# The scaling of a finished sum moved amid the fourth group's relus, and a last stage whose normalise precedes the seventh block's output rows

## Chip, cores and metric

The kernel runs on one core of a Trainium2 chip. The metric is the device time of one execution in microseconds (us), the median of several runs. Everything is fp32 unless said otherwise.

## What is computed

x has 4096 rows (tokens) of 128 values; adj is a 4096 x 4096 matrix. Four residual branches follow each other:

```python
x = x + gnn0(layernorm(x), adj)          # two layers of a normalised graph aggregation
x = x + ffn0(layernorm(x))               # 8 experts, top-1 routing, capacity 640
x = x + adj @ (layernorm(x) * W)         # third stage: one plain aggregation
h = relu(layernorm(x) @ Wi.T + bi)       # fourth: 64 segments of 64 tokens
for l in range(2):                       # each segment has one expert of 16
    h = relu(h @ Ws[l] + bs[l] + h @ Wr[l, e].T + br[l, e] + h)
x = x + h @ Wo.T + bo
```

The change is in the last stage of the kernel, which computes the last two branches together.

## The kernel before, in words

Each engine has its own program, written out by hand; they are tied together by semaphores only. Nothing is planned by a scheduler, so the order on each engine is the order in the code. TensorE's instructions run in program order, and so do those of VectorE (DVE), ScalarE (ACT), GpSimd (POOL) and SyncE (SP), which starts most DMAs.

In the last stage the 4096 tokens are cut into NB = 8 blocks of BW = 512. For each block k (1 to 8 here) the kernel aggregates columns of adj over all 4096 rows into the PSUM bank PA[1]; scales the sum by W while it copies it to SBUF (`oT`); turns it to token rows with four 128 x 128 transposes (`turn_sum`, bank T[0]); adds the residual (`x3`), takes the moments, normalises (`hn3`); turns it back (`turn_hn3`); computes h0; runs two routed layers; and projects out (`out_proj`) to give rows that are stored to `out`.

The aggregation of blocks 1 to 7 (numbers of `split_block`) uses a 2 x 2 scheme with seven products: `first_pairs`, `cross_pairs`, `right_pairs`, `left_pairs`, each over four quarters of the block's 8 MB. VectorE makes the combinations of matrix blocks that they stream (`sum_forms`, `cross_forms`, `second_forms`, `third_forms`), and after the last quarter it makes one more addition (`add_outer`), which a few small products on TensorE (`select`) put into PA[1]. `select` of block k runs after `first_pairs` of the first quarter of block k + 1. After it come `cross_pairs`, and then `right_pairs` of block k + 1, which starts a new sum in PA[1] and so waits (on `s_oT`) until ScalarE has taken out the finished one.

Work on two blocks is interleaved: while block k is aggregated, the routed layers of the block before it run between its quarters. The routed layers work in four groups g of four segments: groups 0 and 1 are layer 0, groups 2 and 3 are layer 1. `routed` makes the products of a group into one bank of LB = [SR, SM, O[0], O[1]]; VectorE copies them to SBUF (`raw_rows`, L1542), TensorE transposes them (`turn_routed`, L2149) into T[0] for even and T[1] for odd groups, and ScalarE applies bias and relu (L847), two instructions for each of the 16 segments n, since each has the bias of its own expert, whose number ScalarE loads first (L841). The scaling of the finished sum (L828) is ScalarE's first instruction of the next step, behind all 16 segments. `out_proj(k)` waits for these relus (`s_l`).

The last step (`last3` on TensorE, `last_hn3` on VectorE, `last_inputs` on ScalarE) has no next block to hide behind. It works in two halves of 256 tokens: `select`, the scaling by VectorE (L1566) in two halves, `turn_sum_half` into T[0] and T[1], addition (L1571) and moments on VectorE, the power for 1/sqrt on GpSimd (L875, L878), the normalise (L1580), `turn_hn3_half` (L2089), ScalarE's copy (L801), `h0_half` (L2095), ScalarE's relu into `h_a` (L805), then the two layers (`layer`, L2140) and the last `out_proj` (L2162). `keep_warm` issues products whose results nobody reads. Between the turned sum and the normalise stand, for the seventh block, `out_proj(NB - 1)` on TensorE and `out_rows3(NB - 1)` (L1672) on VectorE; the latter releases GpSimd's store of those rows (L974), and GpSimd's addition of the output bias (L979) comes behind that store.

SyncE loads the quarters of adj (L446, 2 MB each) and 16 expert matrices for each block (L642, 256 KB each) as TensorE releases the buffers.

Of the kernel before, what the change touches and what calls it, by code (L numbers as in the profile page):

```python
# [25 lines left out]
ALU = mybir.AluOpType  # L26
# [5 lines left out]
P = 128  # L32
# [51 lines left out]
def build(nc, A, out):  # L84
    ctx = ExitStack()
    with ctx:
# [121 lines left out]
        def x3_of(k):  # L208
            return (x3_even, x3_odd)[k % 2]
# [54 lines left out]
        def turned(k, g, pair, m):  # L264
            if k == NB:
                return (T, PA)[g % 2][m][:, pair * P:(pair + 1) * P]
            return T[g % 2][:, (pair * KH + m) * P:(pair * KH + m + 1) * P]

        b_last = small[:, 48:48 + L2 * KH * SB].rearrange("p (lm s) -> p lm s", lm=L2 * KH, s=SB)
        raw = [U[:, KH * BW + BW * i:KH * BW + BW * (i + 1)] for i in range(2)]  # L270

# [412 lines left out]
        def _(act):  # L684
# [112 lines left out]
            def last_inputs():  # L797

                for h in range(2):
                    act.wait_ge(s_hn3p, NB + h)  # L800
                    nc.scalar.copy(hT3[:, h * HW:(h + 1) * HW], T[h][:, h * HW:(h + 1) * HW]).then_inc(s_hT3, 1)  # L801
                for h in range(2):
                    act.wait_ge(s_h0p, NB + h)
                    for m in range(KH):
                        last = nc.scalar.activation(h_a[:, m * BW + h * HW:m * BW + (h + 1) * HW], O[h][:, m * HW:(m + 1) * HW],  # L805
                                                    ACT.Relu, bias=b_i[:, m:m + 1])
                    last.then_inc(s_h0, 1)
                for g in range(NG):
                    act.wait_ge(s_la, g + 1)
                    alone(act)  # L810
                    rows = group_rows(g, 0)
                    nc.scalar.activation(rows, rows, ACT.Relu).then_inc(s_l, 1)

            def step3(k, slot, rnd, prev, nxt):

                if not prev:

                    for s in range(SB):
                        e = act.value_load(route_sb[0:1, ds((NB - 1) * SB + s, 1)], min_val=0, max_val=E2 - 1)
                        last = nc.scalar.copy(b_last[:, :, s:s + 1], b_r.rearrange("p (lm e) -> p lm e", lm=L2 * KH, e=E2)[:, :, ds(e, 1)])  # L820
                    last.then_inc(s_bl, 1)
                    return
                if k == NB:
                    last_inputs()
                    return
                act.wait_ge(s_agg3, k)
                act.wait_ge(s_oTt, k)
                nc.scalar.activation(oT, PA[1][:, :], ACT.Copy, scale=w_g[:, 0:1]).then_inc(s_oT, 1)  # L828
                act.wait_ge(s_hn3p, k)
                nc.scalar.copy(hT3, T[1][:, :]).then_inc(s_hT3, 1)  # L830
                act.wait_ge(s_h0p, k)
                for m in range(KH):
                    last = nc.scalar.activation(h_a[:, m * BW:(m + 1) * BW], O[m][:, :], ACT.Relu, bias=b_i[:, m:m + 1])
                last.then_inc(s_h0, 1)
                for n in range(L2 * SB):
                    l, s = n // SB, n % SB
                    dst = (h_b, h_a)[l]
                    if n == SB and k in SPLIT:
                        act.wait_ge(s_cross, k)
                        nc.scalar.copy(Eh, PA[0][:, 0:SW]).then_inc(s_e, 1)  # L840
                    e = act.value_load(route_sb[0:1, ds((k - 1) * SB + s, 1)], min_val=0, max_val=E2 - 1)  # L841
                    if s % SH == 0:
                        act.wait_ge(s_rt, (k - 1) * NG + n // SH + 1)
                        alone(act)
                    for m in range(KH):
                        src = turned(k, n // SH, s % SH // 2, m)[:, s % 2 * SEG:(s % 2 + 1) * SEG]
                        last = nc.scalar.activation(dst[:, m * BW + s * SEG:m * BW + (s + 1) * SEG], src, ACT.Relu,  # L847
                                                    bias=b_r[:, ds(e + (l * KH + m) * E2, 1)])
                    if s % SH == SH - 1:
                        last.then_inc(s_l, 1)  # L850
# [144 lines left out]
        def _(dve):  # L995
# [563 lines left out]
            def last_hn3():  # L1559

                x3 = x3_of(NB)
                dve.wait_ge(s_agg3, NB)
                alone(dve)
                for h in range(2):
                    at = slice(h * HW, (h + 1) * HW)
                    nc.vector.tensor_scalar(oT[:, at], PA[1][:, at], w_g[:, 0:1], None, ALU.mult).then_inc(s_oT, 1)  # L1566
                for h in range(2):
                    at = slice(h * HW, (h + 1) * HW)
                    dve.wait_ge(s_oTt, NB + 1 + h)
                    alone(dve)  # L1570
                    nc.vector.tensor_tensor(x3[:, at], T[h][:, at], R[:, ds((NB - 1) * BW + h * HW, HW)], ALU.add)  # L1571
                    dve.drain()
                    stats(lambda t: x3[:, t * D:(t + 1) * D], (h + 1) * H2, h * H2).then_inc(s_mv4, 1)
                out_rows3(NB - 1)
                for h in range(2):
                    dve.wait_ge(s_rstd4, NB + h)
                    alone(dve)
                    for t in range(h * H2, (h + 1) * H2):
                        c = slice(t * D, (t + 1) * D)
                        last = nc.vector.tensor_scalar(hn3[:, c], x3[:, c], mv8[:, t, 0:1], rstd[:, t:t + 1], ALU.subtract, ALU.mult)  # L1580
                    last.then_inc(s_hn3, 1)
                dve.wait_ge(s_bl, 1)
                alone(dve)
                for l in range(L2):
                    for g in (2 * l, 2 * l + 1):
                        raw_rows(NB, g)
                    for g in (2 * l, 2 * l + 1):
                        relu_rows(NB, g)
# [75 lines left out]
            def out_rows3(k):  # L1664
                dve.wait_ge(s_x3b, k)
                alone(dve)
                if k > 1:
                    dve.wait_ge(s_stored, (k - 1) * 16)
                    alone(dve)
                dve.wait_ge(s_fin, k)  # L1670
                alone(dve)
                nc.vector.tensor_tensor(ob, SR[:, :], x3_of(k), ALU.add).then_inc(s_out, 1)  # L1672
                dve.drain()

            def split_step(k):
# [54 lines left out]
        def _(pe):  # L1730
# [347 lines left out]

            def turn_sum_half(h):
                pe.wait_ge(s_oT, NB + 2 + h)  # L2080
                pe.wait_ge(s_l, (NB - 1) * NG - 1 + h)
                for t in range(h * H2, (h + 1) * H2):
                    last = nc.tensor.transpose(T[h][:, t * P:(t + 1) * P], oT[:, t * P:(t + 1) * P], ident[:, :])
                last.then_inc(s_oTt, 1)

            def turn_hn3_half(h):
                pe.wait_ge(s_hn3, NB + h)
                for t in range(h * H2, (h + 1) * H2):
                    last = nc.tensor.transpose(T[h][:, t * P:(t + 1) * P], hn3[:, t * P:(t + 1) * P], ident[:, :])  # L2089
                last.then_inc(s_hn3p, 1)  # L2090
# [29 lines left out]
            def routed(k, g):  # L2120

                l, half = g * SH // SB, g % (SB // SH)
                src = (h_a, h_b)[l]
                if g == 0:
                    pe.wait_ge(s_h0, k)
                    pe.wait_ge(s_out, k)
                elif g == 1 and k == NB:
                    pe.wait_ge(s_h0, NB + 1)
                if l == 1:
# [22 lines left out]
            def out_proj(k):  # L2152
                if k < NB:
                    pe.wait_ge(s_l, k * NG)
                for t in range(BT):
# [3 lines left out]
                    for kk in range(KH):  # L2159
                        for h in range(2):  # L2160
                            at = kk * BW + t * P + h * HC
                            mm = nc.tensor.matmul((T[t // 2] if k == NB else SR)[h * HC:(h + 1) * HC, t * D:(t + 1) * D], h_a[:, at:at + HC],  # L2162
                                                  w_o[:, kk * D:(kk + 1) * D], start=kk == 0, stop=kk == KH - 1)
                    if t == BT - 1 or k == NB and t == 1:
                        mm.then_inc(s_fin, 1)
# [2 lines left out]
            def layer(k, l):  # L2168
                routed(k, 2 * l)
                routed(k, 2 * l + 1)  # L2170

            def split_block(k):
# [31 lines left out]
                cross_pairs(k, 3)  # L2204
                layer(k, 1)
                right_pairs(k, 3)
                turn_routed(k, 2)
                turn_routed(k, 3)
                left_pairs(k, 3)

            def last3(k):
                select(NB - 1)
                turn_sum_half(0)
                turn_sum_half(1)
                out_proj(NB - 1)
                keep_warm(1, S[:, 0:BW], PA[0])
                turn_hn3_half(0)
                keep_warm(1, S[:, 0:BW], PA[0])
                turn_hn3_half(1)
                h0_half(0)  # L2220
                h0_half(1)
                layer(k, 0)
                turn_routed(k, 0)
                turn_routed(k, 1)
# [78 lines left out]
```

## Time and profile before

| | |
|---|---|
| median of 3 runs | 1010.72 us (1010.53 to 1011.39) |
| the profiled execution: its time, its span | 1009.27 us, 1007.5 us |
| mean granted clock of TensorE | 0.99 of 2.4 GHz |
| last stage, aggregation of seven blocks | from about 700 to 979 us of the span |
| a block in its steady state | 40.8 us, TensorE busy 39.45 us |
| from the start of the last two layers to the end | 990.89 to 1007.5 us |

The span runs from the first to the last instruction of the profiled execution; times in the rows count from its start. A busy time is that of the engine's instructions; TensorE's matmuls overlap in the records, and one matmul of fp32 shows as two records. PEld is the load of weights into TensorE. The idle time in brackets behind a row is that of the engine ahead of this instruction, with what ended it. SR, SM, T, O and PA are PSUM banks.

### The profile page before, as it was taken

What the parts mean: (1) busy time and instruction counts of PE and PEld (TensorE: products, weight loads), DVE (VectorE), ACT (ScalarE), POOL (GpSimd) and SP (SyncE); (2) the same over time, 40 slices, a digit from 0 to 9 for tenths busy, and PEclk for the clock granted to TensorE, in tenths of its full rate; (3) what the DMA queues carried; (4) which work ended last, traced back from release to release, by engine and by line L of the source; (5) the groups of instructions that cost most, each with busy time, mean ns of one, the idle gap of its engine ahead of it and who ended that gap; (6) DMA issues with size and microseconds to landing.
All of it is one profiled execution on the core that took longest, in us unless ns stands there. A gap on an engine that the chain in (4) does not pass through costs nothing.

```text
span 1007.5 us, 15493 instructions
## 1 busy us (share of the span) xinstructions
PE 977.2 (97%) x4946; PEld 565.9 (56%) x4946; DVE 496.7 (49%) x1458; ACT 310.3 (31%) x606; POOL 188.8 (19%) x216
## 2 busy tenths in 40 slices
PE   8999999999999999999998999989999999999988
PEld 4555555555555444444444588735666666666655
DVE  6323233223223243344343487676775765756634
ACT  3654654654641010000000244322223223132231
POOL 3110010010010121212221156551120120201101
PEclk9999999999999999999999899989999999999998
DMA  9995685375204698888878259349989898898650
GB/s 358 421 408 180 283 334 206 139 324 230 105 0 168 255 335 309 313 313 320 310 265 329 81 179 297 119 155 365 375 318 336 293 342 305 320 327 292 233 168 23
DMA packets 64479, 262.74 MB, mean 261 GB/s; under 512 B 8836, under 2 KB 24904, under 8 KB 52102
## 3 DMA queue, kind: packets, MB, share of 16 engines
q1 hardware_dynamic: 61254, 257.16, 68.2%
q0 software_dynamic: 2864, 4.39, 1.3%
q8 instruction: 39, 0.64, 0.3%
q14 instruction: 50, 0.41, 0.1%
q10 hardware_dynamic: 272, 0.13, 0.0%
HBM read 243.85 MB, written 20.01 MB: 262 GB/s over the span
## 4 chain that ended last, share of the span: by engine, by line
PE 83%; DVE 4%; ACT 3%; issue 3%; ACTq 2%; DMA 2%; DVEq 2%; POOL 1%; SPq 0%; POOLq 0%
PE PA L1768 22%; PE PA L1788 22%; PE PA L2025 13%; PE O L1963 3%; PE O L2140 3%; PE O L1837 3%; ACTq L841 2%; ACT U L778 2%; PE SR L2162 1%; PE O L1809 1%; PE SR L2140 1%; PE SM L2140 1%; PE O L1799 1%; PE O L2117 1%; PE T L2149 1%
## 5 line engine op out<-in xcount | busy, mean ns | idle before, releaser
L1788 PE MATMUL PA<-ring,S 128*128 128x512 f32 x512 | 229.9, 595 | 1.7 <-DMA ring<-in_adj_cols 1.7
L1768 PE MATMUL PA<-ring,U 128*128 128x512 f32 x512 | 226.7, 595 | 0.0
L1768 PEld LDWEIGHTS PA<-ring,U 128*128 128x128 f32 x512 | 94.8, 190 | 106.6 <-issue 106.5
L1788 PEld LDWEIGHTS PA<-ring,S 128*128 128x128 f32 x512 | 95.2, 190 | 103.2 <-issue 100.4
L2026 PE MATMUL PA<-ring 128*64 128x256 f32 x560 | 133.0, 381 | 0.0
L698 ACT ACTIVATE work<-ring 128x2048 int8<-128x2048 f32 x64 | 122.2, 1910 | 8.9 <-issue 4.7
L2025 PE MATMUL PA<-ring,S 128*64 128x256 f32 x448 | 105.3, 380 | 0.3 <-DVE ring L1626 0.3
L2025 PE MATMUL PA<-ring 128*64 128x256 f32 x336 | 82.5, 382 | 7.8 <-ACT work L828 7.8
L2025 PEld LDWEIGHTS PA<-ring,S 128*64 128x64 f32 x448 | 60.5, 137 | 35.4 <-issue 6.4
L2026 PEld LDWEIGHTS PA<-ring 128*64 128x64 f32 x560 | 75.0, 137 | 0.0
L2025 PEld LDWEIGHTS PA<-ring 128*64 128x64 f32 x336 | 44.4, 137 | 33.9 <-ACT work L828 10.6
L2026 PE MATMUL PA<-U,S 128*64 128x256 f32 x224 | 54.5, 381 | 0.0
L956 POOL DMA_INDIRECT y_d<-R,work x40 | 45.4, 1134 | 46.0 <-DVE R L1438 35.7
L1184 DVE TENSOR_TENSOR U<-O,b_us 128x256 f32<-128x256 f32 x16 | 6.8, 425 | 90.6 <-PE O L1837 90.6
L875 POOL TENSOR_SCALAR small<-mv 128x4 f32<-128x4 f32 (+1 forms) x9 | 2.1, 234 | 259.2 <-DVE mv L1003 259.2
L1616 DVE TENSOR_TENSOR ring<-ring 128x1024 f32<-128x1024 f32 x28 | 34.2, 1222 | 33.2 <-PE PA L2026 33.0
L944 POOL DMA_INDIRECT disp_d<-work x32 | 31.9, 997 | 94.0 <-DVE work L1360 86.7
L847 ACT ACTIVATE work<-T,work 128x64 f32<-128x64 f32 x112 | 29.0, 310 | 63.4 <-PE T L2149 50.8
L847 ACT ACTIVATE U<-T,work 128x64 f32<-128x64 f32 x112 | 29.1, 310 | 51.8 <-PE T L2149 37.5
L1626 DVE TENSOR_TENSOR ring<-ring 128x1024 f32<-128x1024 f32 x28 | 38.4, 1373 | 2.6
L711 ACT ACTIVATE work<-work,small 128x256 f32<-128x256 f32 x32 | 16.6, 588 | 68.4 <-POOL small L908 68.4
L748 ACT COPY work<-T 128x512 f32<-128x512 f32 x8 | 4.7, 586 | 106.0 <-PE T L1873 106.0
(292 smaller groups left out, 1366.9 us busy)
## 6 DMA issues: line engine op xcount, KB each, us to landing
ring<-in_adj_cols SPq DMA_DIRECT2D x52, 2048.0 KB, 8.7
ring<-in_adjT_cols SPq DMA_DIRECT2D x32, 2048.0 KB, 8.7
ring<-w_d SPq DMA_DIRECT2D x128, 256.0 KB, 3.9
ring<-in_adj_cols SPq DMA_DIRECT2D x8, 1024.0 KB, 13.1
ring<-in_Wr SPq DMA_DIRECT2D x4, 2048.0 KB, 9.4
w_d<-ring SPq DMA_DIRECT2D x8, 1024.0 KB
work<-in_w SPq DMA_DIRECT2D x16, 256.0 KB
disp_d<-U SPq DMA_DIRECT2D x4, 650.0 KB, 20.0
```

The costliest lines, as they stand in the source:

```text
L698: last = nc.scalar.activation(junk, src, ACT.Gelu, scale=GELU_SCALE, accum_out=csum[slot][:, col:col + 1])
L847: last = nc.scalar.activation(dst[:, m * BW + s * SEG:m * BW + (s + 1) * SEG], src, ACT.Relu, bias=b_r[:, ds(e + (l * KH + m) * E2, 1)])
L944: nc.gpsimd.indirect_dma_start(disp_d, bass.IndirectOffsetOnAxis(ap=idx[:, t:t + 1], axis=0), rows[:, t * ROW:(t + 1) * ROW], None, bounds ...
L956: nc.gpsimd.indirect_dma_start(y_d, bass.IndirectOffsetOnAxis(ap=e_idx[par][:, q:q + 1], axis=0), e_y[par][:, q * D:(q + 1) * D], None, bo ...
L1616: nc.vector.tensor_tensor(S1[c % 2], q21, q22, ALU.add).then_inc(s_form, 1)
L1626: nc.vector.tensor_tensor(S2[c % 2], S1[c % 2], q11, ALU.subtract).then_inc(s_form, 1)
L1768: mm = nc.tensor.matmul(out_T[:, :], X[:, t * D:(t + 1) * D], ring[slot][t // HT][:, (t % HT) * BW:(t % HT + 1) * BW], start=n == 0, stop= ...
L1788: mm = nc.tensor.matmul(PA[k % 2][:, :], S[:, t * D:(t + 1) * D], ring[slot][t // HT][:, (t % HT) * BW:(t % HT + 1) * BW], start=t == 0, s ...
L1837: mm = nc.tensor.matmul(o, h1T[:, f * BW + t * P:f * BW + (t + 1) * P], W_us[:, f, :], start=f == 0, stop=f == KH - 1)
L2025: nc.tensor.matmul(bank[0:HC, cols], low, low_in, start=start, stop=False, skip_group_check=True)
L2026: return nc.tensor.matmul(bank[HC:P, cols], high, high_in, start=start, stop=False, skip_group_check=True)
L2140: mm = nc.tensor.matmul(LB[g][c * SEG:(c + 1) * SEG, pair * DH:(pair + 1) * DH], src[:, kk * BW + s * SEG:kk * BW + (s + 1) * SEG], wst[n0 ...
```

## The change

1. On ScalarE the scaling of the sum of block k + 1 (numbers of ScalarE's steps) is now issued in step k, ahead of segment n = 14 of 16, so two segments' relus come behind it. Step 1 issues its own at its head.
2. In the seventh block `left_pairs` of the last quarter goes ahead of the transposes of groups 2 and 3.
3. In the last step `turn_sum_half` writes O[0] and O[1] in place of T[0] and T[1] and no longer waits for the relus of the seventh block; `turn_hn3_half` has that wait now.
4. `out_proj(NB - 1)` moves behind `h0_half(1)`, with its result in PA[0] in place of SR; `out_rows3(NB - 1)` moves behind the normalise; the keep-warm products write PA[1], and there are three in place of one ahead of the first `turn_hn3_half`.
5. h0 of the last step goes to a buffer of its own, `h_last`, since `out_proj(NB - 1)` still reads `h_a`; and the first routed products of the last step no longer wait for the seventh block's output rows.

```diff
+        h_last = ring[1][0][:, 0:KH * BW]
...
-                        last = nc.scalar.activation(h_a[:, m * BW + h * HW:m * BW + (h + 1) * HW], O[h][:, m * HW:(m + 1) * HW],
+                        last = nc.scalar.activation(h_last[:, m * BW + h * HW:m * BW + (h + 1) * HW], O[h][:, m * HW:(m + 1) * HW],
...
+            def scaled_sum(k):
+                act.wait_ge(s_agg3, k)
+                act.wait_ge(s_oTt, k)
+                nc.scalar.activation(oT, PA[1][:, :], ACT.Copy, scale=w_g[:, 0:1]).then_inc(s_oT, 1)
...
-                act.wait_ge(s_agg3, k)
-                act.wait_ge(s_oTt, k)
-                nc.scalar.activation(oT, PA[1][:, :], ACT.Copy, scale=w_g[:, 0:1]).then_inc(s_oT, 1)
+                if k == 1:
+                    scaled_sum(1)
...
+                    if n == L2 * SB - SH // 2 and k + 1 < NB:
+                        scaled_sum(k + 1)
...
-                    nc.vector.tensor_tensor(x3[:, at], T[h][:, at], R[:, ds((NB - 1) * BW + h * HW, HW)], ALU.add)
+                    nc.vector.tensor_tensor(x3[:, at], O[h][:, at], R[:, ds((NB - 1) * BW + h * HW, HW)], ALU.add)
...
-                out_rows3(NB - 1)
                 for h in range(2):
                     dve.wait_ge(s_rstd4, NB + h)
...
                     last.then_inc(s_hn3, 1)
+                out_rows3(NB - 1)
...
-                nc.vector.tensor_tensor(ob, SR[:, :], x3_of(k), ALU.add).then_inc(s_out, 1)
+                nc.vector.tensor_tensor(ob, (PA[0] if k == NB - 1 else SR)[:, :], x3_of(k), ALU.add).then_inc(s_out, 1)
...
             def turn_sum_half(h):
                 pe.wait_ge(s_oT, NB + 2 + h)
-                pe.wait_ge(s_l, (NB - 1) * NG - 1 + h)
...
-                    last = nc.tensor.transpose(T[h][:, t * P:(t + 1) * P], oT[:, t * P:(t + 1) * P], ident[:, :])
+                    last = nc.tensor.transpose(O[h][:, t * P:(t + 1) * P], oT[:, t * P:(t + 1) * P], ident[:, :])
...
             def turn_hn3_half(h):
                 pe.wait_ge(s_hn3, NB + h)
+                pe.wait_ge(s_l, (NB - 1) * NG - 1 + h)
...
-                    pe.wait_ge(s_out, k)
+                    pe.wait_ge(s_out, min(k, NB - 1))
...
                 right_pairs(k, 3)
+                if k == NB - 1:
+                    left_pairs(k, 3)
                 turn_routed(k, 2)
                 turn_routed(k, 3)
-                left_pairs(k, 3)
+                if k < NB - 1:
+                    left_pairs(k, 3)
...
                 turn_sum_half(1)
-                out_proj(NB - 1)
-                keep_warm(1, S[:, 0:BW], PA[0])
+                keep_warm(3, S[:, 0:BW], PA[1])
                 turn_hn3_half(0)
-                keep_warm(1, S[:, 0:BW], PA[0])
+                keep_warm(1, S[:, 0:BW], PA[1])
                 turn_hn3_half(1)
                 h0_half(0)
                 h0_half(1)
+                out_proj(NB - 1)
                 layer(k, 0)
```

## Rows read from the trace of the kernel before

**Rows 1.** The page, section 1: busy us (share of the span), instructions

```profile
PE 977.2 (97%) x4946; PEld 565.9 (56%) x4946; DVE 496.7 (49%) x1458; ACT 310.3 (31%) x606; POOL 188.8 (19%) x216
```

**Rows 2.** Stretches: length, busy us (x) of five engines, clock, DMA share, GB/s

```profile
700.00:736.60 36.60, 35.62 (x312) 22.61 (x310) 25.61 (x36) 10.08 (x35) 4.31 (x3) 1.00 0.98 375
...
899.80:940.60 40.80, 39.45 (x360) 25.69 (x360) 27.33 (x37) 11.02 (x38) 5.28 (x4) 1.00 0.86 313
```

**Rows 3.** The waits from 700 to 980: us in total, times, longest

```profile
PE PA L2025 <- ACT work L828: 7.8, 6, 1.3
```

**Rows 4.** TensorE timeline at a boundary: start, us, engine, line [idle, releaser]

```profile
897.81 0.60 PE L2076 MATMUL PA<-W 128*64 128x256 f32 x4
...
898.89 0.38 PE L2025 MATMUL PA<-ring 128*64 128x256 f32 x1
...
900.58 0.43 PE L2025 MATMUL PA<-ring 128*64 128x256 f32 x1 [1.30 <-ACT work L828]
...
903.05 1.97 PE L2162 MATMUL SR<-work,U 128*64 128x128 f32 x32
```

**Rows 5.** Timeline of ScalarE there

```profile
897.91 0.52 ACT L847 ACTIVATE U<-T,work 128x64 f32<-128x64 f32 x2 [0.26 <-issue]
...
899.43 0.52 ACT L847 ACTIVATE U<-T,work 128x64 f32<-128x64 f32 x2 [0.24 <-issue]
899.84 0.69 ACT L828 ACTIVATE work<-PA,work 128x512 f32<-128x512 f32 x1
```

**Rows 6.** The chain that ended last, there

```profile
899.95 0.59 ACT work L828
```

**Rows 7.** Timeline of VectorE there

```profile
903.27 0.69 DVE L1651 TENSOR_TENSOR work<-T,R 128x512 f32<-128x512 f32 x1 [1.83 <-PE T L2103]
```

**Rows 8.** A quarter's loads (L446) to landing, its last issue and its use

```profile
DMA to landing us min/median/max: 7.2/8.7/11.9
...
939.72 0.36 SPq L446 DMA_DIRECT2D ring<-in_adjT_cols  x1
...
956.16 1.23 DVE L1616 TENSOR_TENSOR ring<-ring 128x1024 f32<-128x1024 f32 x1 [1.18 <-PE PA L2026]
```

**Rows 9.** Timelines of all engines at the end

```profile
974.37 1.09 PE L2149 MATMUL T<-ident,U 128*128 128x128 f32 x8
...
977.98 0.65 PE L2073 MATMUL PA<-W 128*64 128x256 f32 x4 [0.64 <-DVE W L1645]
...
980.36 0.42 DVE L1571 TENSOR_TENSOR work<-T,R 128x256 f32<-128x256 f32 x1 [0.25 <-PE T L2083]
...
981.60 0.66 PE L2083 MATMUL T<-ident,work 128*128 128x128 f32 x2 [1.39 <-ACT U L847]
...
982.40 0.42 DVE L1571 TENSOR_TENSOR work<-T,R 128x256 f32<-128x256 f32 x1 [0.74 <-PE T L2083]
...
984.31 0.70 POOL L878 TENSOR_TENSOR small<-small,neg_half 128x2 f32<-128x2 f32 x1 [0.18 <-POOL small L875]
...
985.79 1.94 PE L1746 MATMUL PA<-S,ident 128*128 128x512 f32 x2
...
988.94 1.89 PE L2095 MATMUL O<-work 128*128 128x256 f32 x8
...
990.89 1.06 PEld L2140 LDWEIGHTS SR<-ring,U 128*64 128x64 f32 x12 [0.47 <-ACT U L805]
...
1003.63 0.42 DVE L1724 TENSOR_TENSOR work<-T,work 128x256 f32<-128x256 f32 x1 [0.36 <-PE T L2162]
```

**Rows 10.** GpSimd's bias addition (L979) and its store (L974) to landing

```profile
L979 POOL TENSOR_TENSOR work<-work x8: 1257/3032/3217, 706.5 to 988.3; 128x512 f32<-128x512 f32 x8
...
DMA to landing us min/median/max: 2.8/8.4/9.3
```

**Rows 11.** Stretches at the end (same columns as in group 2)

```profile
980.00:981.00 1.00, 0.21 (x2) 0.00 (x0) 0.68 (x3) 0.58 (x3) 0.00 (x0) 0.82 0.82 166
...
990.00:1005.00 15.00, 12.79 (x116) 8.68 (x114) 7.36 (x18) 3.34 (x8) 0.00 (x0) 1.00 0.01 2
```

More of the change, by code:

```diff
@@ L2122, in routed @@
                 l, half = g * SH // SB, g % (SB // SH)
-                src = (h_a, h_b)[l]
+                src = (h_last if k == NB else h_a, h_b)[l]
                 if g == 0:
                     pe.wait_ge(s_h0, k)
-                    pe.wait_ge(s_out, k)
+                    pe.wait_ge(s_out, min(k, NB - 1))
                 elif g == 1 and k == NB:
@@ L2161, in out_proj @@
                             at = kk * BW + t * P + h * HC
-                            mm = nc.tensor.matmul((T[t // 2] if k == NB else SR)[h * HC:(h + 1) * HC, t * D:(t + 1) * D], h_a[:, at:at + HC],
+                            mm = nc.tensor.matmul((T[t // 2] if k == NB else PA[0] if k == NB - 1 else SR)[h * HC:(h + 1) * HC, t * D:(t + 1) * D], h_a[:, at:at + HC],
                                                   w_o[:, kk * D:(kk + 1) * D], start=kk == 0, stop=kk == KH - 1)
```

## The prediction

> **What bounds the kernel now.** I read the page first: TensorE is busy 97% of a span of 1007.5 us, and no other engine is above half [rows 1]. Then the stretches of the last stage, one for each block. A block in its steady state takes 40.8 us, TensorE is busy for 39.45 us of it at the full clock (2.4 GHz), and the DMA engines for 86% [rows 2]. So in this stage a microsecond counts only if TensorE waits in it. The list of waits of that stage shows what it waits for: six times for the scaling at L828, 7.8 us in all, 1.3 us each [rows 3]; no other wait in it comes to 1 us. The timeline around one block boundary shows what the reader should see [rows 4]: the selecting products (L2076) end, cross_pairs runs, its last record starts at 898.89 and takes 0.215 us of the array, and right_pairs of the next block, which overwrites the bank that L828 reads, starts only at 900.58. The array therefore loses 900.58 - 898.89 - 0.215 = 1.48 us, a little more than the idle time of 1.3 us that is listed, because matmuls overlap. All six boundaries have this form.
>
> Why L828 is late stands in ScalarE's own rows [rows 5]. At 898.41 (897.81 + 0.60) [rows 4] the sum is complete, but ScalarE still has the relus of the last two segments in front of it (one segment every 0.76 us, the last starts at 899.43), and in the chain L828 does its own work only behind them, from 899.95 to 900.54 [rows 6].
>
> At the end of the kernel the chain is another: it runs through small steps of all engines, and TensorE falls to half its clock (1.2 GHz) there; below.
>
> **The change at the six boundaries.** It moves the scaling ahead of those two segments. Two things must be done by then: the select and the relus of the two segments before. The select ends at 898.41 [rows 4], the relus end at 898.43 (897.91 + 0.52) [rows 5]. They meet almost exactly, so ScalarE neither waits long nor holds the sum back. A handover between the two engines takes 0.04 us (900.54 to 900.58) [rows 4, 6]; with 0.69 us for L828 [rows 5] and one handover each way, right_pairs may start at 898.41 + 0.77 = 899.18. Its slot behind cross_pairs is 898.89 + 0.215 = 899.11. Left over is 0.07 us; gained is 1.48 - 0.07 = 1.4 us a boundary, **8.4 us** in six. Bounds: if L828 overlaps with its predecessor as today (0.59 us), nothing is left over, and 1.48 + 0.05 for the array's restart gives 9.2 us in all; if the wait amid the relus costs 0.2 us more of issue, 7.2 us.
>
> What is queued behind the moved instruction: the last two segments' relus, which out_proj waits for. They end where L828 ends now, at about 900.5, or sooner. TensorE has right_pairs (1.72 us) and the four transposes of turn_sum first; out_proj would come at 903.05 - 1.4 = 901.65 [rows 4]. Margin over 1 us: cost nothing; without that cover it would be at most 0.7 us. VectorE is next in line: it must be through its forms when the turned sum comes, at 903.27 now; of the 1.83 us in which it is idle before that 0.4 us remain, so this holds too [rows 7]. From there VectorE, GpSimd and TensorE keep their distances.
>
> Loads: the quarter that comes last is issued at 939.72 and lands 8.7 us later (11.9 us at worst), by 951.6; VectorE takes it at 956.16 [rows 8]. 4.5 us of margin shrink by 1.4 us, once, since the loads are released by TensorE itself and move with it. The DMA share becomes 0.86 x 40.8 / 39.4 = 0.89, and a stretch at 0.98 and 375 GB/s exists in this kernel [rows 2]. Cost nothing; I take the unchanged distances over the bound of a stage that is held by its loads (a rival below).
>
> **The change at the end.** Times here are on the old axis, before the 8.4 us are taken off.
> First, left_pairs of the seventh block goes ahead of the eight transposes. Today left_pairs ends, VectorE adds, and TensorE waits 0.64 us for it, until 977.98 [rows 9]; after, left_pairs starts 0.09 us before the transposes' start of now (974.37), at 974.28, ends at 976.00, the eight transposes follow and cover VectorE's add until 977.11, and the select starts there: 0.87 us earlier.
> Second, the turned sum goes to the O banks and doesn't wait for the relus. Today its second half starts at 981.60, its addition at 982.40, and GpSimd's powers for it end at 985.01 (984.31 + 0.70) [rows 9]. After: the first half's addition starts at 980.36 - 0.87 = 979.49; with its moments it is 1.3 us of VectorE work (today 980.36 to 981.66, where the 0.74 us of idle time before 982.40 begin), so the second addition starts at 980.8, 1.6 us earlier than now, and the power ends at 983.4.
> Third, out_proj and out_rows3 leave the front. Today out_proj holds TensorE until 985.79, VectorE waits for it and then adds before it normalises, and h0 starts at 988.94, behind the second half's two transposes (0.22 us) [rows 9]. After: the first normalise lies at 982.3 to 982.9, the second at 983.6 to 984.2, the transposes at 984.25. The relus of the seventh block end later by the moved transposes, 981.6 + 1.6 = 983.2, which is in time for that, since the second half of the banks is wanted at 984.25 only. Three keep-warm products of 0.86 us (512 columns, twice the 0.43 us that a product of 256 takes in h0) fill 979.6 to 982.2 under the normalise and cost nothing at full clock. h0 starts at 984.25 + 0.22 = 984.47 and takes 4 x 0.43 = 1.74 us, to 986.2.
> Fourth, out_proj now stands between h0 and the last layer: 32 products at full clock, 1.7 us (1.97 us listed in a steady block, less the 0.27 us that the last one overlaps with what follows) [rows 4], until 987.95, which covers ScalarE's relu of h0 (0.5 us of idle today). The layer starts at 987.97 in place of 990.89 [rows 9]: **2.9 us**. Its bounds at full clock: 1.5 us if each of the seven handovers between engines costs 0.2 us more, 3.2 us if VectorE doesn't leave its gaps.
> Fifth, the seventh block's output rows and their store move from about 986 to 988.1, behind both normalises, and so do GpSimd's store and its bias addition. The store lands in 2.8 us at best and 9.3 us at worst [rows 10], so by 999.2 at the latest; the last layer takes from 990.89 to the end 16.6 us, and its first addition into the buffer comes at 1003.63 - 2.9 = 1000.7 [rows 9]: nothing. The bias addition takes 1.26 us at least and 3.0 us in the median, beside VectorE's work [rows 10]: it can hold the copy of the first raw rows for 1.26 us at most, and TensorE has the second product group (some 1.8 us) to do meanwhile. Nothing; at most 0.5 us, within the bound above.
> The SBUF — State Buffer page of the Trainium skill, section "Who interferes with whom", says that VectorE and GpSimd take their common port pair exclusively for a whole instruction, but that a VectorE instruction with at most one SBUF input outside the two-port modes doesn't contend. The raw copy reads PSUM, so by that rule the 0.5 us above would be 0.
>
> **TensorE's clock at the end.** The granted clock was 0.82 between 980 and 981 [rows 11], so it fell about 980.6; the keep-warm product at 985.79 ran at half of it, h0 at 988.94 at the full one again [rows 9]. Before it fell TensorE had waited 0.64 us at 977.98, and worked 0.21 us in the microsecond from 980; the second turned half waited 1.39 us more [rows 9, 11]. With the change the gap of 0.64 us goes, some 0.7 us for the scaling remain, and the keep-warm products follow at 979.6, so I expect the clock to stay up. The sum above assumes it.
> The page TensorE: Matmul & The Clock Gate of the Trainium skill, section "What's actually happening", has throttled as the default state that activity releases. By that rule too three keep-warm products help, but whether they are enough no row here shows.
>
> **Sum.** 8.4 + 2.9 = 11.3 us. The profiled execution took 1009.27 us for a span of 1007.5 us; it becomes 998.0 us with a span of 996.2 us. The median of the three runs is 1.45 us above the profiled one: 1010.72 - 11.3 = **999.4 us**. The bounds of the terms give 7.2 + 1.5 = 8.7 to 9.2 + 3.2 = 12.4 us: 998.3 to 1002.0 us for this case.
>
> **The rivals.**
> (a) The clock falls all the same at 980.6 [rows 11]. Then one of the three keep-warm products is through, the rest takes about 1.8 us each (985.79 + 1.94 less the overlap) [rows 9], the transposes of the first half come at 984.1, one more keep-warm product ends at 986.3, h0 follows at 986.7, half of it at the low clock, out_proj ends at 990.6. The end gains 0.3 us: 1002.0 us. For it: about 1.5 us of gaps remain between 978 and 983; against: today's were twice that. 13%.
> (b) The scaling waits longer, because the select signals later than its modelled end, and half of the boundary gain goes: 1010.72 - 4.2 - 2.9 = 1003.6 us. Against: TensorE runs only 0.87 us of cross_pairs between the two, so each 0.1 us of lateness costs 0.1 us. 10%.
> (c) The blocks are held by their loads after all and keep 40.8 us: only the end gains, 1007.8 us. For it: the DMA share of 86%; against: no wait of TensorE or VectorE in the stage names a DMA. 5%.
> (d) The other side: the clock falls at 980.6 and doesn't come back before the end. From 990 to 1005 TensorE is busy 12.79 us at the full clock [rows 11], which would double: 1002.0 + 12.8 = 1014.8 us. It decides from 8.7 us of that work done at half clock. Against: today it came back by 988.9, within 9 us. 3%.
> My forecast has 67%; 2% I can't name. A difference of 0.2% is what a measurement of this kernel can tell from no change, 2.0 us here. Faster: 67 + 13 + 10 + 5 less a little, 94%; same 3%; slower 3%. The range takes in the forecast and (a) in full, and stops short of most of (b): 997.8 to 1003.0 us.
>
> **What the profile after would show.** At the boundaries: no wait of right_pairs for the scaling, or under 0.2 us; a block of 39.4 us; L828's successor standing between relus 0.8 us after the second of group four; no new wait of out_proj for relus or of VectorE for a load. At the end: no wait ahead of the select; turned halves 0.45 us apart; a granted clock of 1.00 from 978 on; the last layer starting some 11.3 us before 990.89, at 979.6 of the new axis; from there to the end 16.6 us as now. It would be wrong if the select ended after the second segment's relus, if a form or a load came in the place of the wait, or if the clock fell.

## The result, and the profile after

The changed kernel takes 997.93 us (median of 4 runs, 997.64 to 999.02), the kernel before 1010.62 us beside it (4 runs, 1008.65 to 1011.39). The ratio is 0.988, with a 95% interval from 0.986 to 0.990. The profiled execution took 997.93 us for a span of 996.2 us.

**The block boundaries.** The stretches of the last stage (columns as in [rows 2]), one steady block of the new length, show a TensorE that is busy throughout; the 40.80 us of [rows 2] held 39.45 us of work.

```profile
815.40:854.70 39.30, 39.30 (x362) 25.64 (x360) 27.19 (x37) 10.99 (x38) 5.28 (x4) 1.00 0.89 327
```

The timeline of TensorE around the last boundary, to be held against [rows 4]:

```profile
931.40 0.60 PE L2083 MATMUL PA<-W 128*64 128x256 f32 x4
...
932.48 0.38 PE L2032 MATMUL PA<-ring 128*64 128x256 f32 x1
...
932.79 0.43 PE L2032 MATMUL PA<-ring 128*64 128x256 f32 x1
...
934.67 0.66 PE L2110 MATMUL T<-ident,work 128*128 128x128 f32 x4
935.26 0.55 PE L2169 MATMUL SR<-work,U 128*64 128x128 f32 x6
```

The last record of cross_pairs starts at 932.48, right_pairs at 932.79: 0.31 us, where a record takes 0.215 us. About 0.1 us is left of the 1.48 us. ScalarE's timeline there, against [rows 5]:

```profile
931.51 0.52 ACT L854 ACTIVATE U<-T,work 128x64 f32<-128x64 f32 x2 [0.26 <-issue]
932.05 0.69 ACT L818 ACTIVATE work<-PA,work 128x512 f32<-128x512 f32 x1
932.69 0.52 ACT L854 ACTIVATE U<-T,work 128x64 f32<-128x64 f32 x2
933.45 0.52 ACT L854 ACTIVATE U<-T,work 128x64 f32<-128x64 f32 x2 [0.25 <-issue]
```

The scaling (L818) starts 0.02 us after the relus of the second segment end, and 0.05 us after the select's end at 932.00 (931.40 + 0.60). The two segments behind it end at 933.97, and out_proj starts at 935.26: their cover of over 1 us is there. VectorE's next step waits 0.45 us for the turned sum, against 1.83 us in [rows 7]:

```profile
935.47 0.69 DVE L1658 TENSOR_TENSOR work<-T,R 128x512 f32<-128x512 f32 x1 [0.45 <-PE T L2110]
```

**The end.** Timeline of all engines, against [rows 9]:

```profile
968.57 0.65 PE L2080 MATMUL PA<-W 128*64 128x256 f32 x4
...
970.95 0.42 DVE L1578 TENSOR_TENSOR work<-O,R 128x256 f32<-128x256 f32 x1 [0.25 <-PE O L2089]
971.03 2.74 PE L1753 MATMUL PA<-S,ident 128*128 128x512 f32 x6
...
972.17 0.42 DVE L1578 TENSOR_TENSOR work<-O,R 128x256 f32<-128x256 f32 x1
...
974.09 0.82 POOL L885 TENSOR_TENSOR small<-small,neg_half 128x2 f32<-128x2 f32 x1 [0.18 <-POOL small L882]
...
974.40 0.44 PE L2096 MATMUL T<-ident,work 128*128 128x128 f32 x2 [0.63 <-DVE work L1586]
...
975.99 1.89 PE L2102 MATMUL O<-work 128*128 128x256 f32 x8
...
977.81 1.97 PE L2169 MATMUL PA<-work,U 128*64 128x128 f32 x32
...
979.61 1.90 PE L2147 MATMUL SR<-ring 128*64 128x256 f32 x16
...
981.69 0.69 DVE L1549 COPY U<-SR 128x512 f32<-128x512 f32 x1 [1.06 <-PE SR L2147]
982.07 1.29 POOL L986 TENSOR_TENSOR work<-work 128x512 f32<-128x512 f32 x1
```

The select no longer waits, the three keep-warm products (L1753) take 2.74 us at the full clock, and the last layers start 11.04 us after the select (979.61 - 968.57), where it was 12.91 us. From there to the end it is 16.6 us, as before (16.65 us). The stretch in which most is idle shows the clock, which never leaves 1.00:

```profile
973.00:974.00 1.00, 0.77 (x2) 0.00 (x0) 0.67 (x4) 0.64 (x3) 0.82 (x2) 1.00 0.68 242
```

Where the 11.3 us of span went, by these rows: 0.3 us lie ahead of the first select, where nothing was changed; six boundaries of 1.38 us make 8.28 us (a block goes from 40.76 to 39.38 us, select to select); the earlier select of the seventh block 0.86 us; the steps up to the last layers 1.87 us; the rest nothing.

### The profile page after: what moved, and what is told of

Read it like the earlier page. It is cut to its first block, busy times and chain, and to the rows that moved or that the text cites. A ratio compares the mean times of both kernels' runs of the same rounds, so it can differ in the third digit from the quotient of the medians.

```text
span 996.2 us, 15501 instructions
## 1 busy us (share of the span) xinstructions
PE 975.3 (98%) x4950; PEld 564.8 (57%) x4950; DVE 496.7 (50%) x1458; ACT 311.2 (31%) x606; POOL 189.2 (19%) x216
## 4 chain that ended last, share of the span: by engine, by line
PE 87%; DVE 4%; ACT 2%; issue 2%; DMA 2%; DVEq 2%; POOL 1%; ACTq 0%; SPq 0%; POOLq 0%
PE PA L1775 22%; PE PA L1795 22%; PE PA L2032 16%; PE O L1970 3%; PE O L2147 3%; PE O L1844 3%; ACT U L779 2%; PE O L1816 1%; PE T L2156 1%; PE SM L2147 1%; PE SR L2147 1%; PE O L1806 1%; PE O L2124 1%; PE SR L2169 1%; PE PA L1960 1%
## 5 line engine op out<-in xcount | busy, mean ns | idle before, releaser
L712 ACT ACTIVATE work<-work,small 128x256 f32<-128x256 f32 x32 | 16.6, 589 | 68.4 <-POOL small L915 68.4
```

## The experiments

Ahead of the last stage executions and chips differ: the stage's first product started anywhere from 661.5 to 675.0 us. In the four of these executions that start it latest (672.5 to 675.0 us: e6, e7, e10, e11) the granted clock was also at half for 7 us or more near 650 us (0.50 between 651 and 654 us); in the other ten it was not. So differences of a microsecond are read inside the stage, from the timelines of the profiled executions (one for each kernel), and the medians stand beside them. The edits of e1 and e10 are made to the kernel before, all others to the changed kernel. "Block" is the time from one select to the next; "to the layers" is from the seventh block's select to the first product of the last layers; "stage" is from the stage's first product to the end. All in us.

| kernel | block | last block | to the layers | stage | ratio to before (95%) |
|---|---|---|---|---|---|
| before | 40.76 | 39.84 | 12.91 | 343.3 | |
| changed | 39.38 | 37.60 | 11.04 | 332.2 | 0.988 (0.986 to 0.990) |
| e1 boundaries only | 39.38 | 38.46 | 12.08 | 334.2 | 0.992 (0.991 to 0.994) |
| e2 end only | 40.76 | 38.98 | 11.03 | 340.5 | 0.999 (0.998 to 1.000) |
| e4 one segment later | 40.00 | 38.21 | 11.03 | 336.0 | 0.993 (0.991 to 0.994) |
| e5 two segments earlier | 39.75 | 38.29 | 11.03 | 334.8 | 0.992 (0.990 to 0.994) |
| e3 one keep-warm product | 39.38 | 37.60 | 12.49 | 333.7 | 0.989 (0.987 to 0.992) |
| e6 left_pairs back | 39.38 | 38.47 | 11.03 | 333.1 | 0.991 (0.988 to 0.993) |
| e7 out_proj in front | 39.38 | 37.60 | 13.87 | 335.1 | 0.993 (0.991 to 0.996) |
| e8 out_proj split | 39.38 | 37.60 | 9.46 | 330.6 | 0.987 (0.984 to 0.989) |
| e9 turned into T | 39.38 | 37.60 | 16.07 | 337.2 | 0.996 (0.994 to 0.998) |
| e10 before, kept warm | 40.76 | 39.84 | 11.22 | 341.7 | 0.999 (0.998 to 1.001) |
| e11 changed again | 39.38 | 37.61 | 11.03 | 332.2 | 0.991 (0.989 to 0.994) |
| e12 out_proj split again | 39.38 | 37.60 | 9.46 | 330.7 | 0.989 (0.987 to 0.992) |

**e1, the boundaries alone.** The kernel before, with `scaled_sum` and its calls of the diff's third to fifth pieces and nothing else.

> Only the scaling moves amid the relus; the end of the kernel is that of before. If the gain at the block boundaries and at the end add up as in my sum, this one holds the six boundaries alone: 1.38 us each (a block of 39.38 us in place of 40.76 us), 8.3 us in all, a median some 8.3 us under that of before, and a granted clock that falls near the end as before. Rival: part of the gain needs the other edits (the loads or the end absorb it), then under 6 us.

Each of the six boundaries gives the same 1.38 us as in the changed kernel, with the end left as it was. The blocks' gain stands by itself. A surprise is the end: 12.08 us to the layers in place of 12.91, though nothing was changed there. The clock fell here too, but later against the work and for a shorter time; stretch by stretch:

```profile
973.00:974.00 1.00, 1.00 (x16) 1.00 (x18) 0.81 (x3) 0.00 (x0) 0.79 (x2) 0.78 0.37 141
974.00:975.00 1.00, 1.00 (x14) 1.00 (x12) 0.35 (x3) 0.00 (x0) 0.23 (x1) 0.50 0.00 0
...
976.00:977.00 1.00, 1.00 (x3) 0.43 (x2) 0.69 (x1) 0.00 (x0) 0.00 (x0) 0.52 0.00 0
977.00:978.00 1.00, 0.84 (x5) 0.29 (x4) 0.94 (x4) 0.00 (x0) 0.56 (x1) 1.00 0.00 0
```

In the kernel before, the same end of the program had it at half from 980.6 (0.82 in [rows 11]) to 987.5:

```profile
981.00:982.00 1.00, 0.41 (x2) 0.28 (x2) 0.59 (x4) 0.45 (x2) 0.14 (x1) 0.50 0.89 297
...
987.00:988.00 1.00, 1.00 (x5) 0.42 (x4) 1.00 (x4) 0.00 (x0) 0.69 (x1) 0.77 0.00 0
```

That is 3.4 us at half, from 4.6 us after the select, against 6.8 us, from 2.7 us after it; out_proj took 3.1 us in place of 3.7. So one and the same end can differ by 0.8 us through the place where the clock falls. Both numbers are of one execution each, and what sets that place isn't shown.

**e2, the end alone.**

```diff
-                if k == 1:
-                    scaled_sum(1)
+                scaled_sum(k)
...
-                    if n == L2 * SB - SH // 2 and k + 1 < NB:
-                        scaled_sum(k + 1)
```

> Everything but the moved scaling. My sum gives 0.86 us for the earlier select and 2.7 us for the steps up to the last layers with the clock up, some 2.7 to 3.5 us under before, with blocks of 40.76 us and the wait of 1.3 us back six times. Rival: the whole time comes from the blocks and the end is worth under 1 us.

The waits of the stage have the old one back (the line numbers are those of this kernel):

```profile
PE PA L2029 <- ACT work L818: 7.8, 6, 1.3
```

The stage is 2.8 us shorter than before, where the sum had 2.9 us. The medians show 1.4 us (1006.64 against 1008.05 us), which is within 0.2%: alone, this part couldn't have been told from no change by its time.

**e4, the scaling one segment later.**

```diff
-                    if n == L2 * SB - SH // 2 and k + 1 < NB:
+                    if n == L2 * SB - 1 and k + 1 < NB:
```

> The changed kernel with the scaling ahead of the last segment in place of the last two. My theory: the scaling comes 0.76 us later, right_pairs waits 0.76 us more at each of six boundaries: 4.5 us slower than the changed kernel, a block of 40.1 us. Rival (the select is what it waits for, and there is slack behind it): under 1.5 us slower.

TensorE's timeline at the first boundary: right_pairs waits again.

```profile
733.15 0.38 PE L2032 MATMUL PA<-ring 128*64 128x256 f32 x1
...
734.09 0.43 PE L2032 MATMUL PA<-ring 128*64 128x256 f32 x1 [0.56 <-ACT work L818]
```

Its slot was 733.37, so 0.72 us are lost in place of 0.1 us. A block is 0.62 us longer, 3.8 us in six. The segment costs a little less than its 0.76 us, since the scaling now overlaps with the relu ahead of it (4.5 us were expected). There is no slack behind the scaling; the rival is out.

**e5, two segments earlier.**

```diff
-                    if n == L2 * SB - SH // 2 and k + 1 < NB:
+                    if n == L2 * SB - SH and k + 1 < NB:
```

> The changed kernel with the scaling ahead of all four segments of group four. My theory: it is held by the select then, which ends 0.04 us before the second segment's relus do, so right_pairs gains nothing (0 to 0.05 us), while four segments' relus stand behind it and end 1.5 us later, 0.3 us after the time at which out_proj starts now: 0.3 us a boundary, 1.6 us slower than the changed kernel. Rival (the wait for the select costs nothing behind it): the same time as the changed kernel within 0.5 us.

ScalarE's timeline, and TensorE's behind it:

```profile
735.46 0.69 ACT L818 ACTIVATE work<-PA,work 128x512 f32<-128x512 f32 x1 [1.65 <-PE PA L2083]
...
738.46 0.52 ACT L854 ACTIVATE U<-T,work 128x64 f32<-128x64 f32 x2 [0.24 <-issue]
```

```profile
739.03 1.97 PE L2169 MATMUL SR<-work,U 128*64 128x128 f32 x32 [0.30 <-ACT U L854]
```

ScalarE stands for 1.65 us in front of the scaling, right_pairs starts no sooner, and four segments' relus end at 738.98, for which out_proj waits. That costs 0.37 us at each of five boundaries and 0.69 us at the sixth, where out_proj waits 0.62 us: 2.6 us in the stage, more than the 1.6 us expected. This is the wait that takes the place of another, and it appears as soon as the scaling is moved ahead of what produces its input. The place chosen in the change, between segments n = 13 and n = 14, is the best of the three tried (one segment earlier was not run), and what is left (0.1 us) is the chain select, scaling, right_pairs.

**e6, left_pairs behind the transposes again.**

```diff
                 right_pairs(k, 3)
-                if k == NB - 1:
-                    left_pairs(k, 3)
                 turn_routed(k, 2)
                 turn_routed(k, 3)
-                if k < NB - 1:
-                    left_pairs(k, 3)
+                left_pairs(k, 3)
```

> The changed kernel with the seventh block's left_pairs behind the transposes again. My sum: TensorE waits 0.64 us for VectorE's addition again and the select comes 0.86 us later, while the relus come 1.7 us earlier than now, which nothing needs: 0.9 us slower than the changed kernel. Rival: the step is hidden under the normalise, then no difference.

```profile
980.45 0.65 PE L2080 MATMUL PA<-W 128*64 128x256 f32 x4 [0.64 <-DVE W L1652]
```

The wait for VectorE's addition is back in TensorE's timeline, the last block is 0.87 us longer, and the rest is as long as with the change. That term of the sum is confirmed.

**e3, one keep-warm product in place of three.**

```diff
-                keep_warm(3, S[:, 0:BW], PA[1])
+                keep_warm(1, S[:, 0:BW], PA[1])
```

> The changed kernel with one keep-warm product in place of three ahead of the first normalised half's transposes; TensorE stands idle for some 2.5 us there. If the three products keep the clock up (my reading), the granted clock falls to half near 973 and the end costs 2 to 4 us more. Rival: the clock was kept by the shorter gaps alone, then the same time, since the products lie under the normalise.

The stretches of it, one after the other:

```profile
978.00:979.00 1.00, 0.00 (x0) 0.00 (x0) 0.73 (x4) 0.76 (x4) 0.80 (x2) 1.00 0.80 197
979.00:980.00 1.00, 0.20 (x2) 0.21 (x3) 0.60 (x2) 0.76 (x4) 0.74 (x2) 1.00 0.26 100
980.00:981.00 1.00, 1.00 (x4) 0.27 (x2) 0.55 (x2) 0.40 (x2) 0.30 (x1) 0.77 0.00 0
981.00:982.00 1.00, 1.00 (x4) 0.87 (x4) 0.05 (x1) 0.02 (x1) 0.00 (x0) 0.50 0.00 0
```

TensorE stands for 2.35 us, and the granted clock falls to half (1.2 GHz) behind it. The way to the layers is 1.45 us longer, less than the 2 to 4 us expected: the steps up to h0 take 0.35 us more, h0 itself 1.10 us more (2.92 in place of 1.82 us to out_proj's start), and by out_proj, 0.7 us after the slow time of 3.4 us, the clock is back. So it is the products under the normalise that keep the clock up: it stays at 1.00 in all eight profiled executions in which three of them, or two and half of out_proj, come under the normalise with no wait of over 1 us ahead (changed, e2, e4, e5, e6, e8, e11, e12), and falls in this one.

**e7, out_proj in front again.**

```diff
                 turn_sum_half(1)
-                keep_warm(3, S[:, 0:BW], PA[1])
+                out_proj(NB - 1)
+                keep_warm(1, S[:, 0:BW], PA[1])
...
                 h0_half(1)
-                out_proj(NB - 1)
```

> The changed kernel with the seventh block's out_proj ahead of the normalised halves' transposes again, and one keep-warm product behind it. My theory: out_proj waits for the relus until 974.7, so the transposes come 2.9 us later and the last layers 1.0 us later than now, and if the clock falls in the gap of 3.6 us, 3 to 5 us later. Rival: its place doesn't matter, since it is done once either way: no difference.

```profile
984.42 3.26 PE L2169 MATMUL PA<-work,U 128*64 128x128 f32 x32 [3.51 <-ACT U L854]
```

TensorE waits 3.51 us for the relus, out_proj then runs for the most part at half clock (3.26 us in place of 1.97), and the layers start 2.83 us later, a little under the 3 to 5 us expected with a fallen clock.

**e9, the turned halves in T again.**

```diff
             def turn_sum_half(h):
                 pe.wait_ge(s_oT, NB + 2 + h)
+                pe.wait_ge(s_l, (NB - 1) * NG - 1 + h)
...
-                    last = nc.tensor.transpose(O[h][:, t * P:(t + 1) * P], oT[:, t * P:(t + 1) * P], ident[:, :])
+                    last = nc.tensor.transpose(T[h][:, t * P:(t + 1) * P], oT[:, t * P:(t + 1) * P], ident[:, :])
```

VectorE reads T[h] in place of O[h] too.

> The changed kernel with the turned halves in the T banks again, behind the relus of groups three and four. My theory: the second turned half waits until 974.7 on the changed kernel's axis in place of 970.7, its addition starts 3.1 us later, and with the clock up the last layers 3.1 us later, with a fallen clock 4 to 6 us. Rival: the normalise is held by GpSimd's powers and not by the banks, then under 1 us.

```profile
978.85 0.66 PE L2090 MATMUL T<-ident,work 128*128 128x128 f32 x2 [3.00 <-ACT U L854]
979.30 4.64 PE L1753 MATMUL PA<-S,ident 128*128 128x512 f32 x6
```

The second half waits 3.00 us for the relus, and the three keep-warm products then take 4.64 us in place of 2.74, at half clock and on the path. 5.0 us later in all. With left_pairs ahead of the transposes the O banks are needed: the one edit makes the relus late, and the other takes them off the path.

**e10, the kernel before, only kept warm.**

```diff
                 select(NB - 1)
+                keep_warm(1, S[:, 0:BW], PA[0])
                 turn_sum_half(0)
+                keep_warm(2, S[:, 0:BW], PA[0])
                 turn_sum_half(1)
```

> The kernel before with three more keep-warm products, one ahead of the first turned half and two between the turned halves, and nothing else. If the clock alone is most of what the end gained, out_proj takes 1.8 us in place of 3.7 there, the normalise comes 1.5 to 2 us earlier, and from select to the last layers it takes 10.5 to 11.5 us in place of 12.9. If the order is what counts (the turned sum that waits for the relus, out_proj on the path), under 1 us of the 1.9 us comes back. Should the clock fall all the same, the run tells nothing on this.

A stretch in it, and TensorE's timeline:

```profile
990.00:991.00 1.00, 1.00 (x11) 0.65 (x12) 0.37 (x3) 0.00 (x0) 0.50 (x2) 1.00 0.71 236
```

```profile
990.52 1.97 PE L2162 MATMUL SR<-work,U 128*64 128x128 f32 x32
```

The clock stays at 1.00, out_proj takes 1.97 us in place of 3.68, and the layers come 11.22 us after the select. That is 1.69 of the 1.87 us which the whole new order reached, with three products that nobody reads. It is one profiled execution; the medians (1012.54 against 1013.20 us) differ by less than can be told from no change.

**e8, e12: out_proj split, with the changed kernel beside it (e11).** The first half of the seventh block's out_proj takes the place of one keep-warm product, the second half that of the other.

```diff
-            def out_proj(k):
+            def out_proj(k, lo=0, hi=BT):
                 if k < NB:
-                    pe.wait_ge(s_l, k * NG)
-                for t in range(BT):
+                    pe.wait_ge(s_l, k * NG - (hi < BT))
+                for t in range(lo, hi):
...
-                keep_warm(3, S[:, 0:BW], PA[1])
+                out_proj(NB - 1, 0, H2)
+                keep_warm(2, S[:, 0:BW], PA[1])
                 turn_hn3_half(0)
-                keep_warm(1, S[:, 0:BW], PA[1])
+                out_proj(NB - 1, H2, BT)
                 turn_hn3_half(1)
                 h0_half(0)
                 h0_half(1)
-                out_proj(NB - 1)
```

> A step further: the seventh block's out_proj in two halves, the first in place of the first keep-warm product (its tokens' relus are done by 971.3), the second in place of the keep-warm product between the two normalised halves' transposes. My theory: 1.7 us of products leave the path between h0 and the last layers, which then wait for ScalarE's relu of h0 instead (0.3 us): 1.4 to 1.7 us faster than the changed kernel. Rival: the second half waits for the relus of group four (done at 974.7) and holds the transposes of the second half, then a gain under 0.8 us.

> The changed kernel once more, beside the split one on the same chip, since chips and executions differ by several us ahead of the last stage: blocks of 39.38 us, 11.04 us from select to the last layers, 16.6 us from there to the end.

> The split out_proj once more: 9.46 us from select to the last layers, and so 1.5 us under the changed kernel of the same call, in the stage's own times and, less sharply, in the medians. Rival: the gain seen once was chance, then the medians agree within 0.5 us.

The timeline of e12:

```profile
980.17 1.10 PE L2169 MATMUL PA<-work,U 128*64 128x128 f32 x16
...
981.47 1.89 PE L2102 MATMUL O<-work 128*128 128x256 f32 x8
...
983.43 0.87 PE L2147 MATMUL SR<-ring 128*64 128x256 f32 x6
```

Both halves fit where the keep-warm products were, h0 follows, and the layers start 1.96 us behind h0's start in place of 3.62. It was 9.46 us to the layers both times, 1.57 us less than in e11. The medians beside each other are 1001.63 and 1004.63 us (6 runs each): they agree in sign, but the difference of 3.0 us is more than the stage holds. In its last stage this version is faster than both kernels.

## Why the prediction was right, point by point

- **The bound.** Only TensorE's waits counted in the steady blocks. Six waits went, and each block shrank by 1.38 us: what the array had lost from start to start (1.48 us) less the 0.1 us left, not the idle time that the list gives (1.3 us).
- **The six boundaries.** 8.4 us predicted, 8.28 us measured. Left over was 0.1 us in place of 0.07 us. The two conditions that meet at one instant, select and relus, do so in the trace after as well, and e4 and e5 show that one segment later costs 0.6 us a boundary and two segments earlier 0.4 us or more. Rival (b) didn't come: the select signals within 0.05 us of its listed end.
- **What stands behind the scaling.** The cover of over 1 us was there; e5 took it away and had the wait for the relus at once. VectorE's 0.4 us was 0.45 us.
- **The loads.** No wait names them; the DMA share went from 0.86 to 0.89 as worked out. Rival (c) is out.
- **The earlier select.** 0.87 us predicted, 0.86 us measured, and by e6 alone.
- **The steps to the layers.** 2.9 us with the select, 2.73 us measured. Out_proj took 1.8 us on the path in place of 1.7, and h0 started 0.06 us later than worked out. The store and the bias addition cost nothing: the copy of the first raw rows (981.69, 0.69 us) ran for 0.31 us beside the bias addition (982.07, 1.29 us), and neither took longer than in e7, where they lie apart (0.69 and 1.29 us). So the rule cited from the Trainium skill, SBUF — State Buffer, "Who interferes with whom", agrees with this trace.
- **The clock.** It stayed up, against rivals (a) and (d), and e3 shows by which edit: the keep-warm products. The rule cited from the Trainium skill, TensorE: Matmul & The Clock Gate, "What's actually happening", that activity releases the throttle, agrees with both: 0.50 in e3, 1.00 in the changed kernel and in e10.
- **What the prediction had wrong in its reasons.** It booked the 2.05 us between select and layers to the order (O banks, out_proj and out_rows3 out of the front) and took the clock as a condition. The old times from which it subtracted were times at half clock: out_proj's end at 985.79 is one. e10 shows that the old order with the clock up comes within 0.18 us of the new one. (Rival (a) held the same: with a fallen clock it left only 0.3 of the 2.9 us.) So the new order as such is worth little in that stretch; what the change removed there is the slow time, and out_proj was put on the path between h0 and the layers, where e8 shows that 1.57 us of it could have been saved. The sum was right because either way the same microseconds go.
- **The medians.** The ratio gives 12.2 us (10.5 to 13.9), the profiled spans 11.3 us, the stage 11.1 us. The sum of 11.3 us lies within the interval, and the profiled execution came out as worked out: 997.93 us, forecast 998.0. The median was forecast at 999.4 us, by adding the 1.45 us by which the median before stood above its profiled run. That term didn't carry over: after the change the median is the profiled run's own time. So the measured 997.93 us lies only 0.1 us inside the lower end of the range (997.8 us), and that it lies inside is luck; it says nothing on the mechanism. Measured again (e11), the same change gave 8.7 us by its ratio (6.2 to 11.2), with a stage of 332.2 us as here. The rest is the spread ahead of the stage; the fall of the clock near 650 us, named with the table, goes with the four latest starts, and why the others differ no run here was aimed at.

## What to carry to other kernels

Move an instruction that another engine waits for up to the point where its own input is ready, and not beyond: count what it then stands behind and what stands behind it, and check both by moving it either way. When a step's old time is subtracted in a sum, look at the clock it was taken at; an idle stretch that costs nothing by its own length, since it lies under another engine's work, can cost through the clock (1.45 us in e3), and useful work that is due soon is a better filler than products nobody reads. Where the stages ahead of a change vary by more than the change is worth, compare the changed stage's own times.

## What the runs showed of the hardware

TensorE's granted clock fell to half 0.7 us after it had stood for 2.35 us in e3, and after the gaps of 0.64 and 0.70 us and amid the one of 1.39 us of [rows 9]; it stayed at 1.00 across the gaps of 0.70 and 0.63 us of the changed kernel. With the same end of the program it was at half for 6.8 us in the kernel before and for 3.4 us in e1, so the price of the same gaps differed by 0.8 us.
